# Perceiver block: cross attention's exponentials, reciprocals and encoding a slot later in their engines' order, and the last statistics ahead of the last outputs

## The reference

```python
xn, mn = _rmsnorm(x, rms_scale), _rmsnorm(mem_seq, rms_scale)
q = _apply_rope(einsum('BTD,NDH->BTNH', xn, q_w), q_pos) * HEAD_DIM ** (-0.5)
k, v = einsum('BSD,cKDH->cBSKH', mn, kv_w); k = _apply_rope(k, k_pos)
logits = einsum('BTKGH,BSKH->BKGTS', q, k)              # 4 heads, one K and V
probs = softmax(where(mem_mask, logits, MASK_FILL))
enc = einsum('BKGTS,BSKH->BTKGH', probs, v)
x = x + einsum('BTNH,NHD->BTD', enc, out_w)
```

## Time and profile before

| | us |
|---|---|
| median of 3 runs | 1065.26 (1064.7 to 1065.47) |
| the profiled execution | 1066.37 |
| its span in the profile | 1064.4 |
| PE busy | 930.7 (87%) |
| DVE busy | 668.4 (63%) |
| ACT busy | 505.0 (47%) |
| POOL busy | 375.6 (35%) |

### The profile page before, as it was taken

How to read it: one execution, slowest core, us unless ns; L and a number is a source line. 1 busy time by engine, 2 the same in 40 slices (tenths; PEclk the granted TensorE clock), 3 DMA queues, 4 the chain that set the end, 5 groups by cost and what they waited for, 6 DMA issues and landing times. The chain is left out here.

```text
span 1064.4 us, 22549 instructions
## 1 busy us (share of the span) xinstructions
PE 930.7 (87%) x7307; PEld 700.7 (66%) x7307; DVE 668.4 (63%) x1334; ACT 505.0 (47%) x1059; POOL 375.6 (35%) x506
## 2 busy tenths in 40 slices
PE   3798879898888888878979999999889999999996
PEld 2787667686676776657968887888765444444443
DVE  5577756766766777676366566766656538475543
ACT  4565445654455554544333333433446455555542
POOL 3354444444444444440022111211103325444434
PEclk9899989999999999988989999999989999999998
DMA  6621223211222322331355543444422102012011
GB/s 178 184 76 56 80 88 86 87 54 57 76 86 73 97 74 76 115 115 41 90 160 140 149 126 108 127 124 108 118 60 76 55 1 88 32 40 70 21 60 43
DMA packets 100318, 93.02 MB, mean 87 GB/s; under 512 B 45424, under 2 KB 61904, under 8 KB 100176
## 3 DMA queue, kind: packets, MB, share of 16 engines
q1 hardware_dynamic: 99376, 90.96, 29.2%
q10 hardware_dynamic: 672, 0.26, 0.1%
q0 software_dynamic: 128, 0.03, 0.0%
HBM read 74.37 MB, written 12.66 MB: 82 GB/s over the span
## 5 line engine op out<-in xcount | busy, mean ns | idle before, releaser
L255 PE MATMUL bank<-f,f 128*128 128x256 f32 (+4 forms) x5032 | 637.8, 300 | 68.8 <-issue 26.0
L255 PEld LDWEIGHTS bank<-f,f 128*128 128x128 f32 (+3 forms) x5032 | 460.9, 160 | 196.5 <-issue 80.8
L244 DVE TENSOR_TENSOR f<-bank,f 128x512 fp32r<-128x512 f32 x211 | 140.5, 683 | 47.7 <-ACT f L241 45.8
L241 ACT ACTIVATE f<-bank 128x512 fp32r<-128x512 f32 x211 | 121.1, 591 | 88.8 <-PE bank L230 83.6
L230 PE MATMUL bank<-f,f 128*128 128x128 f32 x896 | 132.5, 279 | 33.7 <-DVE f L244 13.0
L230 PEld LDWEIGHTS bank<-f,f 128*128 128x128 f32 x896 | 102.9, 143 | 56.1 <-issue 31.3
L1248 PE MATMUL bank<-f,f 128*128 128x512 f16 x512 | 123.1, 384 | 0.0
L1221 POOL TENSOR_TENSOR f<-f,f 128x512 f32<-128x512 f32 x59 | 75.1, 1273 | 132.9 <-ACT f L1216 132.9
L1226 DVE SCALAR_TENSOR_TENSOR f<-bank,f,f 128x512 f16<-128x512 f32 x64 | 48.0, 750 | 92.0 <-ACT f L1208 75.8
L463 POOL TENSOR_TENSOR f<-f,f 128x512 f32<-128x512 f32 x32 | 42.0, 1311 | 160.9 <-ACTq L75 138.9
L954 POOL TENSOR_TENSOR f<-f,f 128x512 f32<-128x512 f32 x32 | 33.4, 1043 | 177.4 <-DVE f L951 177.4
(11 more groups left out here) (138 smaller groups left out, 995.6 us busy)
## 6 DMA issues: line engine op xcount, KB each, us to landing
f<-in_ctx_dram SPq DMA_DIRECT2D x71, 256.0 KB, 2.8
f<-x_scratch SPq DMA_DIRECT2D x64, 256.0 KB, 3.8
x_scratch<-f SPq DMA_DIRECT2D x32, 256.0 KB, 2.0
f<-in_L_ffn_W_fc_dram SPq DMA_DIRECT2D x32, 256.0 KB, 2.9
f<-in_L_ffn_W_proj_dram SPq DMA_DIRECT2D x32, 256.0 KB, 3.4
f<-in_x_dram SPq DMA_DIRECT2D x31, 256.0 KB, 2.9
f<-in_ktab_dram SPq DMA_DIRECT2D x71, 64.0 KB, 2.0
f<-f SPq DMA_DIRECT2D x64, 64.0 KB, 2.4
```

The source lines that it names most:

```text
L241: return maybe("act", lambda e: e.activation(hi, src, ACT.Copy), sem(name + "_hi"), waits, when)
L244: return maybe("dve", lambda e: e.tensor_tensor(lo, src, hi.bitcast(F32), ALU.subtract), sem(name + "_lo"), waits, when)
L255: f = lambda e, i=i, a=a, b=b: e.matmul(dst, a, b, start=(first and i == 0), stop=(last and i == n - 1), skip_group_check=check)
```

## The change

It makes three moves in the cross attention and one in the tail. (a) `stage_exp` goes from order 6 of slots 4b+10 and 4b+11 to order 2 of slots 4b+11 and 4b+12. (b) The reciprocals leave it and become `stage_rden`, order 2 of slot 4b+13. (c) The split of `enc` leaves `stage_PV` (slot 4b+17, order 7) and becomes `stage_et`, order 3 of slot 4b+18. (d) In the last slot the statistics come ahead of all matmuls of the last two `s3_p` (four stood before them), with the squares ahead of the sums and a wait for each of the two; behind them the row tiles follow one after another, each with both steps. No instruction is added or left out.

```diff
@@ -514,9 +514,11 @@
                                               accum_out=den[:, u, t:t + 1]),
                 sem("s_exp"), [*done["nm", b], *d("rden", b - 2)])
         done["exp", b] = [te]
-        if t == 1:
-            done["rden", b] = [op("dve", lambda e: e.reciprocal(rden[:, u, :], den[:, u, :]),
-                                  sem("s_rden"), [te, *d("rbT", b - 2)])]
+
+    def stage_rden(b):
+        u = b % 2
+        done["rden", b] = [op("dve", lambda e: e.reciprocal(rden[:, u, :], den[:, u, :]),
+                              sem("s_rden"), [*done["exp", b], *d("rbT", b - 2)])]
 
     def stage_R(b):
 
@@ -560,10 +562,13 @@
             te = op("dve", lambda e: e.tensor_tensor(enc[:, :], bank[NE][:, 0:256], rb[:, :], ALU.mult),
                     sem("s_enc"), [tk, *done["rb", b], *d("et", b - 1)])
             done["enc", b] = [te]
-            o = (b % 2) * 64
-            done["et", b] = split("s_et", enc[:, :].rearrange("p (n t) -> p n t", n=4),
-                                  ETh[:, b // 2 % 2, :, o:o + 64], ETl[:, b // 2 % 2, :, o:o + 64],
-                                  [te, *d("o", b // 2 - 2)])
+            at(b * FT + 18, 3, lambda: stage_et(b))
+
+    def stage_et(b):
+        o = (b % 2) * 64
+        done["et", b] = split("s_et", enc[:, :].rearrange("p (n t) -> p n t", n=4),
+                              ETh[:, b // 2 % 2, :, o:o + 64], ETl[:, b // 2 % 2, :, o:o + 64],
+                              [*done["enc", b], *d("o", b // 2 - 2)])
 
     def stage_O(i):
         terms = []
@@ -709,9 +714,10 @@
         at(s0 + 6, 4, lambda b=b: stage_KT(b))
         for t in range(2):
             at(s0 + 9 + t, 5, lambda b=b, t=t: stage_LG(b, t))
-            at(s0 + 10 + t, 6, lambda b=b, t=t: stage_exp(b, t))
+            at(s0 + 11 + t, 2, lambda b=b, t=t: stage_exp(b, t))
             at(s0 + 14 + 2 * t, 2, lambda b=b, t=t: stage_PT(b, t))
             at(s0 + 15 + 2 * t, 7, lambda b=b, t=t: stage_PV(b, t))
+        at(s0 + 13, 2, lambda b=b: stage_rden(b))
         at(s0 + 14, 5, lambda b=b: stage_R(b))
         if b % 2:
             at(s0 + 21 if b + 1 < nb else s0 + 19, 8, lambda b=b: stage_O(b // 2))
@@ -1264,23 +1270,22 @@
                 give(kp[t], [te])
 
     def s3_plast():
-        for t in (2, 3):
-            s3_p(last - 1, [t])
         for t in range(4):
-            s3_p(last, [t])
+            for q in (last - 1, last):
+                s3_p(q, [t])
 
     def s3_stat(g):
         v, k = g % 2, take()
-        w = [*tok["acc", g], *tok["acc2", g], *gfree[k], t_on]
-        for t in range(4):
-            for z in range(2):
+        w = {1: [*tok["acc2", g], *gfree[k], t_on], 0: tok["acc", g]}
+        for z in (1, 0):
+            for t in range(4):
                 rows = slice(t * 128, (t + 1) * 128)
                 parts = [acc[:, v, z, rows]] + ([sq3[:, last % 2, rows]] if z and g == ng - 1 else [])
                 for n, a in enumerate(parts):
                     tk = op("pe", lambda e, t=t, z=z, a=a, n=n, m=len(parts) - 1: e.matmul(
                         bank[k][:, z * 4 + t:z * 4 + t + 1], a, ones[:, 0:1], start=n == 0, stop=n == m,
-                        skip_group_check=True), sem("f_p") if t == 3 and z and n == len(parts) - 1 else None,
-                        w if t + z == 0 else ())
+                        skip_group_check=True), sem("f_p") if t == 3 and not z else None,
+                        w[z] if t + n == 0 else ())
         tok["stat", g] = [tk]
         D_ = lambda f, w: op("dve", f, sem("f_dv"), w)
         free = [t for j in range(4) for t in d2("fin", g - 1, j)]
@@ -1389,7 +1394,6 @@
         if q < last - 1:
             at(H0 + q + 2, 2.5, lambda q=q: s3_p(q))
     at(H0 + last + 2, 2.5, s3_plast)
-    at(H0 + last + 2, 2.1, lambda: s3_p(last - 1, [0, 1]))
     for g in range(ng):
         at(H0 + 16 * g + 16 + 1, 2.2, lambda g=g: s3_stat(g))
     at(B2 + 30, 4.6, s3_scale)
```

## The result

The changed kernel took 1049.83 us (median of 4 runs, 1047.34 to 1050.4) beside 1064.98 for the kernel before on the same chip (1063.77 to 1065.47): a ratio of 0.9855, 95% interval 0.9837 to 0.9873, or 15.2 us less. Forecast were 1062.2, in a range that ended at 1057.5. The profiled execution took 1049.8 us, its span is 1047.9 after 1064.4.

A forecast was written before the change was run, and what follows sets the result against it. TensorE was taken to pace the cross attention, the gain lying in its idle time. -1.2 + 3.1 - 2.0 - 1.6 - 0.7 - 0.7 = -3.1 us gave 1062.2 against the median (1063.3 from the profiled execution); range 1057.5 to 1066.5.

The forecast's parts named there:

- Q1 rounds: Cross-attention rounds with the query's first part: K's rest split no longer behind the negation (0.08 us), fifteen waits, -1.2 us.
- Q2 rounds: Cross-attention rounds with the query's second part: encoding's split delays TensorE's transposes, 0.34 us in nine rounds, +3.1 us.
- weighted sum: Six TensorE waits at its second half shrink once the reciprocal comes a slot later: -2.0 us, bounds 0 and -3.2.
- end of the stage: waits: Cross attention's last slots: -1.6 us at the wait of 479.84 and -0.7 at that of 501.48.
- end of the stage: clock: Output projection at 479.84 shorter by up to 2.1 us if shorter waits keep the clock up; left out, a bound.
- tail: Statistics start with the last sum, not behind it, so the last output comes 0.7 us earlier: -0.7 us.
- The 122 us of idle time: ScalarE's waits (56.4, 36.1 us) and VectorE's (29.1), on engines that do not pace the stage: not the gain.
- the -1.6: Middle taken for TensorE's wait at 479.84, between gains of 0.7 and 2.4 us.
- the better end: VectorE's split of 477.31 gets in front of the GpSimd step, releasing TensorE at 479.84 earlier: 2.4 us gained.
- The wait at 501 us: TensorE's 1.66 us wait for a weight split behind an exponential: -0.7 us, bounds 0 and -1.6; sign: under 1 us.
- The race for the port: VectorE's split of 477.31 against a GpSimd step on a shared SBUF port: gain 0.7 us lost, 2.4 won.
- The case of all sixteen matmuls at half clock: Tail's last output matmuls take 7.2 us, ending 1.8 late: +1.1 there, whole -1.3, 1064.0; a quarter of the forecast's 0.52.

The follow-up runs named there:

- (d) alone: Kernel before with only the tail's new order of statistics and output matmuls: 1063.57 us, one run.
- (c) alone: Kernel before with only the encoding's split a slot later: 1065.22 us, ratio 0.9996.
- (b) alone: Kernel before with only the reciprocals moved to slot 4b+13: 1059.81 us, ratio 0.9949.
- (a) alone: Kernel before with only the negation and exponentials a slot later, reciprocals still behind the second exponential: 1053.14 us, ratio 0.9888.
- the four programs with those rounds: Kernel before (1064.98 us), and it with only the tail's move (1063.57), with extra matmuls (1062.35), or with late exponentials for the last four batches (1061.97).
- the two series of the changed kernel: The changed kernel measured twice, unaltered, against the kernel before: 1049.83 us (ratio 0.9855) and 1051.36 us (0.9871).

## Why the prediction was wrong

The direction and most mechanisms were right; the size was wrong by 12 us. Term by term, in TensorE's waits from (d) alone to the changed kernel (neither has half clock in the rounds):

| step | forecast | measured |
|---|---|---|
| Q1 rounds | -1.2 | -3.4 |
| Q2 rounds | +3.1 | 0.45 (0.1 of it shows as a wait) |
| weighted sum (forecast for six waits, thirteen there) | -2.0 | -5.0 (the six: -3.3) |
| one wait at the spread of the reciprocals | none | -0.4 |
| end of the stage: waits | -2.3 | -1.7 to -2.0 |
| end of the stage: clock | 0 (bound -2.1) | -0.7 to -1.7; by itself -1.9 |
| busy time (clock) in the steady rounds | none | -0.1 to -5.2 between two profiles |
| tail | -0.7 | -0.7 |

**The Q2 rounds are the step that failed, by two sizes.** The prediction put the encoding's split, 0.42 us, and the negation, 0.08, on the chain that releases TensorE's transposes, in nine rounds. The chain is right, in eight rounds: there the transposes start 0.15 us behind the end of K's split, in the kernel before, in the changed one and in (c) alone. Both sizes are wrong. The encoding's split held K's split, and the transposes with it, by 0.25 us, not 0.42, since a VectorE instruction starts before the row of the one ahead of it ends (0.34 behind it in the row), and the rest was lost in other gaps. The negation was worth 0.20, not 0.08: it waits for the semaphore of the maximum's second instruction, the read of the accumulator, and K's split need not. So 0.25 - 0.20 = 0.05 us is what arrives in a round, and 0.06 is measured: 0.45 us in place of 3.1. The same 0.20 in place of 0.08 sets the Q1 rounds (13 waits by 0.20 and one by 0.77 make 3.4), and the negation put back returns it in both kinds of round.

The Trainium skill draws the line that the sizes turn on (VectorE: DVE Perf Modes, Two Vector instructions with no wait between them): it tells instructions that are held for all earlier ones from those that start before these have ended, and counts the accumulator's read as an instruction of its own. The 0.34 agrees, and the read has a row of its own at 334.91. What holds the negation in this trace is the program's semaphore: it starts at 335.03, 0.04 us after that read has ended.

**The weighted sum** went past its bound (-3.2). The six waits that were counted gave -3.3 by themselves: 2.1 us are left of 5.5, where I had kept 3.5. Seven more of the same step gave the other 1.7: three of them (1.1 us) in the row of 4.7 us that names VectorE and that I had left out, the others mostly under "issue". What made them late is shown in part. Either (a) or (b) alone shortens these waits, and either takes most or all of the reciprocal's wait away (29.1 us; 4.4 in (a) alone, none in (b) alone), so the reciprocal fits as the cause that the prediction named. ScalarE's first splits, held behind an exponential, were late too: 42.2 us of VectorE's waits, 5.3 in the changed kernel. This row stood in the trace and I did not ask who pays for it. But (b) alone leaves it at 42.2 us and shortens the waits all the same, and (c) alone takes 13.5 us of it away together with two of the waits (0.58 and 0.75 us), so what it cost TensorE by itself is not shown. The 122 us of idle time of the earlier trace rows I had called "not the gain"; part of it was. By idle time the parts add up: 5.5 for (a), 3.1 for (b), 0.2 for (c), against 9.0 for all.

**The end of the stage** came out near its sum. The step that the -1.6 is about, the output projection, starts 12.2 us behind the matmul at 465.02 (now 453.16) in place of 14.8: 2.6 us earlier, beyond the 2.4 named for the better end. The rope's first product (L465) starts 2.3 us earlier, where 1.7 was the estimate, and takes 0.43 us in place of 0.73. The wait ahead of the projection, forecast to shrink by 1.6, still grew by 1.66, because the waits ahead of it shrank by 1.1 and 1.3 us and the clock had not fallen yet (it fell at 465.1 now and at 470.8 before), so that TensorE came earlier still. The releaser is not the split of 477.31 itself but the skipped step queued behind it. The wait at 501 us went to 0.27, under the 1 us named. The race for the port, for which the Trainium skill has the rule (SBUF — State Buffer, Who interferes with whom), gave nothing: the split took 1.09 in place of 1.75 us and the product ahead of it 1.49 in place of 0.83, 2.58 us together in both kernels. Since a wait follows, what the clock gives ahead of the projection only lengthens that wait; the two rows of the table divide one sum.

**The clock** was left out of the sum, and that was its second fault. At the end of the stage it is worth 1.9 us alone, near the bound of 2.1. In the steady rounds I had not looked for it: 10.2 us of half clock stood in the profiled execution before, and going by the four programs with those rounds it is at least partly the execution's. How much of the 15.2 us it makes is not settled: the two series of the changed kernel differ by 1.5 us, with the same waits.

**The tail** was right to 0.02 us. The case of all sixteen matmuls at half clock, which the Trainium skill's rule was read to make the likely one (TensorE: Matmul & The Clock Gate, What's actually happening), did not come: they took 3.61 us, 0.226 each, where 0.224 was worked out for the full clock. The clock fell only behind them, at 1042.0.

## What to carry to other kernels

Price each instruction on a chain by the distance between starts, not by its row: here 0.42 us were worth 0.25 and 0.08 were worth 0.20. Where TensorE's row shows no wait in brackets, compare its distance to the releaser, and to the start of the matmul ahead, over several rounds and kernels; the bracket counts from a modelled end. A row of a list of waits may shrink because its waits stand under another name: lay two traces side by side, wait by wait. Idle time of engines that don't set the pace is worth following all the same, one wait at a time, to the wait of the engine that does; here queue order on ScalarE and VectorE was worth 9 us to TensorE. Compare idle time between the same two instructions of two traces and the granted clock apart: the first repeats between executions, the second need not.

## What the runs showed of the hardware

Two executions of one program, with the same idle time of TensorE within 0.1 us in each stage, had 0 and 3.4 us of half clock in the steady rounds and 3.4 and 6.8 at the end of the stage. The Trainium skill says of the start of a kernel that the number of matmuls at the lower clock varies from run to run (TensorE: Matmul & The Clock Gate, What's actually happening). These two agree in the start-up, with 6.8 us of half clock at 35.0 in one and 3.4 at 36.6 in the other, and here it varies in the middle of the kernel too. A stretch of 3.4 us cost 1.2 us where TensorE had little idle time behind it (at 395.0); at 266.0 the 1.1 us that it cost came back whole, since TensorE waited 1.1 us less right behind it.

A step skipped by a branch still stands in its engine's queue: TensorE waited 3.96 us for one that did no work itself, until VectorE was through with the split queued ahead of it.

VectorE's extra 16 us are the rope's products. The largest group in the steady rounds, before and after (line, form, count, busy us, mean ns):

```profile
L467 DVE TENSOR_TENSOR f<-f,f 128x256 f32<-128x256 f32 x29 | 23.5, 812 | 0.0
```

```profile
L467 DVE TENSOR_TENSOR f<-f,f 128x256 f32<-128x256 f32 x29 | 42.9, 1479 | 0.0
```

The same 29 products take 1479 ns in place of 812, since VectorE now waits for the same eviction of K and V as GpSimd's product (L463) and starts beside it. The port rule named above agrees. It is 19 us more on L467, 9 more on L471 and 6.6 less on L465 (their rows overlap, so 16 in busy time). At least in one place TensorE waits behind it:

```profile
257.44 0.43 DVE L465 SCALAR_TENSOR_TENSOR f<-f,f 128x256 f32<-128x256 f32 x1 [1.49 <-ACTq L75]
257.78 1.52 DVE L467 TENSOR_TENSOR f<-f,f 128x256 f32<-128x256 f32 x1
...
261.34 0.97 PE L251 MATMUL bank<-f,f 128*128 128x256 f32 x6 [0.90 <-DVE f L244]
```

From the product of 1.52 us on, VectorE works without a longer pause than 0.24 us through two rest splits, the second of which releases TensorE. What that costs over all rounds was not measured.
